# Value product of a key block cut in two halves of its query columns, in an attention and expert kernel on one Trainium2 core

## The chip, the cores and the metric

The kernel runs on one core of one Trainium2 chip. The metric is the device time of one execution in microseconds (us); lower is better. TensorE (PE in the profile) does the matrix products, PEld is its weight load, VectorE is DVE, ScalarE is ACT, GpSimd is POOL, SyncE is SP (SPq is its queue of DMA issues).

## What is computed

`x` is 8 x 1024 tokens of 256 numbers. It is normalised, and three things are added: the input, an attention layer, and a feed-forward layer of eight experts (two chosen per token) with one shared expert. The change lies in the attention. Cut to that:

```python
xn = layernorm(x)
Q, K, V = [(xn @ W + b).reshape(8, 1024, 16, 16) for W, b in ((Wq, bq), (Wk, bk), (Wv, bv))]
scores = einsum('bqhd,bkhd->bhqk', Q, K) * 16 ** -0.5 + alibi       # alibi: slope of the head * (k - q)
attn = softmax(scores, axis=-1)
out = einsum('bhqk,bkhd->bqhd', attn, V).reshape(8, 1024, 256) @ Wo + bo
y = x + out + experts(xn) + shared(xn)
```

## The kernel before

All five engines run the same walk through the work, `Order.run` (L78): each engine's class overrides the steps in which it has something to do, and semaphores tie them together. So the order in which `Order` calls the steps is the order of instructions on each engine.

**Stages.** First the tokens are normalised and projected (16 groups of 512 tokens, up to about 225 us). Then comes the attention, then the experts in 71 blocks of 256 tokens, then the shared expert with the output projection.

**The attention** goes over 64 pairs: a pair `r` is two heads of one batch entry (8 entries, 16 heads). A pair has 8 key blocks `kc` of 128 keys, and `attention(s, n)` with `s = 8 * r + kc` is called for each; it issues work on every second call, for two key blocks at once, by the string `ORDER` (L42). I call the work of one key block a **step**. Its letters:

- `S`, `scores` (L567): one product of 128 keys by 512 queries, 54 rows deep, for one head `hh` and one half `half` of the 1024 queries. Head 0 sits in rows 0 to 53 of the operands (`QO`, `KO`, both parts of the tile OPS), head 1 in rows 64 to 117. Four `S` per step fill PSUM banks 0 to 3; ScalarE's `exp` (L772) takes two banks at once and writes a 128 x 1024 tile of probabilities into `pta` or `ptb`. A score product of half `n` waits for the `exp` of two halves before, which frees its banks.
- `u`, `max_unit` (L542): one product of 128 queries by 512 keys, 52 rows deep, for the row maxima of a later pair (48 units, 12 steps, ahead). It goes to one of three banks (5, 6, 7) in a ring: `ring_bank` (L528) makes unit `n` wait until VectorE has reduced unit `n - 3` (semaphore `mxred`). VectorE's reduction is L917, four per step. `S` and `u` beside it are for different heads, so for different rows of the array: I call the two a **couple**.
- `P`, `values` (L583): the value product of one key block, two steps behind the scores: four products, one for each head and query half, each 128 keys deep and 32 columns of weights wide, 512 query columns long. Each has its own 32 columns of the array and its own 32 partitions of PSUM bank 4, which sums over the eight key blocks of the pair. The operands are plain 32-bit floats, and every such product stands in the trace as two passes (8 MATMUL records for the four).

The maxima of a pair are finished with a small reduction (L921) and three small GpSimd instructions (L1179, L1182, L1184), transposed on TensorE in `max_rows` (L556, the product of L488) into bank 0, copied by ScalarE (L761) and sent by SP into the operands of the next pair. `max_rows(r + 1)` comes in the two-step call that begins at `kc == 4`; it waits for the `exp` of the first half of key block 5, which frees bank 0. At the end of a pair ScalarE copies bank 4 into `accs` (L779); SP sends the sums of the exponentials to `sq` (L1368), VectorE takes their reciprocals (L926), and SP and GpSimd bring them back and multiply.

The loop of `attention` is the part that the change touches:

```python
ORDER = "SuSuSuSuPSuSuSuSuP"
...
                    if v == 1 and kc == 4 and r + 1 < NPAIR:
                        self.max_rows(r + 1)
                    if s >= 2:
                        self.values(*divmod(s - 2 + v, 8))
                    v += 1
```

Of the kernel before, what the change touches and what calls it, by code (L numbers as in the profile page):

```python
# [20 lines left out]
GT = 512  # L21
# [6 lines left out]
NPAIR = NB * NH // 2  # L28
# [10 lines left out]
PAIR_AT = (3, 6)  # L39
V_AT = 10  # L40
UNITS = (0, 2, 5, 7)
ORDER = "SuSuSuSuPSuSuSuSuP"  # L42
KMAX, KEXP = 52, 54
NPT = 8
SCAT_AT = 34
# [28 lines left out]
class Order:  # L74
# [132 lines left out]
    def attention(self, s, n):  # L207

        r, kc = divmod(s, 8)
        if s % 2 == 0:  # L210
            i = v = 0
            for c in ORDER:
                if c == "S":
                    if r < NPAIR:
                        self.scores(r, kc + i // 4, i % 2, i // 2 % 2)
                    i += 1
                elif c == "u":
                    if n < 32 * NPAIR:
                        self.max_unit(n)
                        n += 1  # L220
                else:
                    if v == 1 and kc == 4 and r + 1 < NPAIR:
                        self.max_rows(r + 1)
                    if s >= 2:
                        self.values(*divmod(s - 2 + v, 8))
                    v += 1
            if kc == 0:
                self.next_pair(r)
            elif r >= 1:
                self.heads(r - 1, kc // 2)  # L230
        if r < NE + 2 and kc == 1:
            self.pack_expert(r)
        if s < NBLK:
            self.clear_slots(s)
        if SCAT_AT <= r < SCAT_AT + NG:
            self.scatter_rows(r - SCAT_AT, kc, 16 * r + 2 * kc)
        if kc == 5 and r % 8 in (2, 3) and r < NPAIR - 8:
            self.load_v(r // 8 + 1, r % 8 - 2)
        if s % 4 == 3:
            self.route(s // 4)  # L240
        return n
# [23 lines left out]
    def load_pair(self, r, i): pass  # L265
    def begin_heads(self): pass
    def scores(self, r, kc, hh, half): pass
    def values(self, r, kc): pass
    def heads(self, r, i): pass
    def pack_expert(self, e): pass  # L270
    def clear_slots(self, s): pass
# [46 lines left out]
def build(nc, t, out):  # L318
    ctx = ExitStack()
    with ctx:  # L320
        sem = {n: ctx.enter_context(nc.semaphore("s_" + n)) for n in SEMS}
# [7 lines left out]
        ps = ctx.enter_context(nc.psum_tensor("ps", [P, 8, 512], F32))  # L329
# [39 lines left out]
        vb = VB[:, :].rearrange("p (b c n) -> p b c n", b=2, c=8)  # L369
# [68 lines left out]
        def pt(n):  # L438
            s = n % NPT
            return pta[:, s, :] if s < NPT // 2 else ptb[:, s - NPT // 2, :]  # L440
# [10 lines left out]
        def projections_over(w):  # L451

            w.wait_ge("lgc", NG)
            w.wait_ge("vmm", 4 * NG)
            w.wait_ge("wol", 1)
            for k in range(2):
                w.wait_ge(f"qh{k}", 16 * NG // 2)
                w.wait_ge(f"ql{k}", 16 * NG // 2)
                w.wait_ge(f"vs{k}", 16 * NG // 2)
            for k in range(3):  # L460
                w.wait_ge(f"xn{k}", 16 * len(range(k, NG, 3)))
# [8 lines left out]
        class Tensor(Order):  # L470
# [109 lines left out]
                if hh == 1:  # L580
                    q.then_inc(sem["smm"], 1)

            def values(self, r, kc):  # L583
                b, j = divmod(r, NH // 2)
                n = 16 * r + 2 * kc
                self.w.wait_ge("exp", n + 2)
                self.w.wait_ge("vcp", 2 * b + 2)
                if kc == 0:
                    self.w.wait_ge("acc1", r)
                    self.w.wait_ge("vev", 4 * NG)  # L590
                for hh in range(2):
                    for half in range(2):
                        g4 = 2 * hh + half
                        q = self.mm(ps[32 * g4:32 * g4 + 32, 4, :],
                                    vb[:, b % 2, kc, 32 * (2 * j + hh):32 * (2 * j + hh) + 32],
                                    pt(n + half)[:, hh * GT:(hh + 1) * GT], kc == 0, kc == 7)
                q.then_inc(sem["pv"], 1)

            def route(self, i):
                if i != 15:  # L600
# [112 lines left out]
        class Scalar(Order):  # L713
# [57 lines left out]
                self.w.wait_ge("smm", n + 1)  # L771
                self.e.activation(pt(n), ps[:, b:b + 2, :], ACT.Exp).then_inc(sem["exp"], 1)  # L772

            def values(self, r, kc):
                if kc == 7:
                    projections_over(self.w)
                    self.w.wait_ge(f"ox{r % 2}", 16 * (r // 2))
                    self.w.wait_ge("pv", 8 * (r + 1))
                    self.e.copy(accs[:, r % 2, :], ps[:, 4, :]).then_inc(sem["acc1"], 1)  # L779
# [699 lines left out]
```

## Time and profile before

| | |
|---|---|
| median of 3 runs | 2723.81 us (2722.07 to 2725.03) |
| the profiled execution | 2719.96 us, span 2717.9 us, mean granted clock of TensorE 0.982 |
| TensorE, matmuls | 2527.5 us busy, 93% of the span |
| VectorE | 2114.4 us, 78% |
| ScalarE | 1639.8 us, 60% |
| GpSimd | 858.1 us, 32% |
| L917, reductions of maxima | 2048, 1270.6 us busy, 681 ns each |
| L475, value products | 4096 records, 555.9 us busy |

"Busy" of an engine is the time in which at least one of its instructions runs. Matmuls are pipelined, so that many overlap; their ends are modelled. The number in brackets behind an instruction is the idle time of its engine before it, and what ended it.

### The profile page before, as it was taken

To read this page: it belongs to the slowest core of one execution; us is meant where nothing else is said; L and a number is where in the kernel's file an instruction comes from. 1 tells how busy PE (TensorE), PEld (TensorE's weight loads), DVE (VectorE), ACT (ScalarE), POOL (GpSimd) and SP (SyncE) were. 2 spreads that over 40 slices of the span, in tenths; PEclk is the share of its full clock that TensorE was granted. 3 is DMA by queue.
4 is the path that set the end of the run, shared out by engine and by line. 5 is a ranking of instruction groups with operands and counts; after the bars stand their busy time and mean duration, and the time that the engine had idled before them with its cause. 6 is when DMAs were issued, how large, how long until landed. Compare 5 with 4: busy or idle time off the path is not lost.

```text
span 2717.9 us, 42994 instructions
## 1 busy us (share of the span) xinstructions
PE 2527.5 (93%) x16090; PEld 1580.8 (58%) x16090; DVE 2114.4 (78%) x3518; ACT 1639.8 (60%) x2314; POOL 858.1 (32%) x920
## 2 busy tenths in 40 slices
PE   4999989999999999998999999899999999999998
PEld 3774333333333333333333333799999988887887
DVE  7887888999999998888899996677777765555544
ACT  2445666777777776776677777677777752232222
POOL 4333434100101104445441001333333333444333
PEclk8998899999999999999999999999999999999999
DMA  5995555222222224444442221577777753344332
GB/s 187 335 324 198 189 180 175 77 62 62 76 60 72 70 62 125 135 131 128 125 120 70 68 65 59 194 241 242 242 239 239 239 170 94 96 117 110 97 93 78
DMA packets 213359, 383.62 MB, mean 141 GB/s; under 512 B 45264, under 2 KB 134544, under 8 KB 203792
## 3 DMA queue, kind: packets, MB, share of 16 engines
q1 hardware_dynamic: 175040, 218.25, 26.2%
q0 software_dynamic: 37024, 161.83, 18.8%
q8 instruction: 128, 2.10, 0.3%
q10 hardware_dynamic: 1088, 0.79, 0.1%
q14 instruction: 79, 0.65, 0.1%
HBM read 248.84 MB, written 141.43 MB: 144 GB/s over the span
## 4 chain that ended last, share of the span: by engine, by line
PE 62%; DVE 22%; issue 6%; ACT 5%; DMA 4%; SPq 1%; POOL 1%; ACTq 0%; DVEq 0%; POOLq 0%
PE ps L475 60%; DVE mx L917 13%; DVE OPS L1088 3%; ACT pta L772 2%; PE ps L488 2%; DVE VB L1085 2%; DMA sq<-accs 2%; ACT OPS L844 1%; SPq L1347 1%; DVE OL L1074 1%; ACT OPS L826 1%; DMA WR0c<-Wd,widx 1%; DVE VB L1105 0%; DVE xn L891 0%; DMA xt<-in_x 0%
## 5 line engine op out<-in xcount | busy, mean ns | idle before, releaser
L917 DVE TENSOR_REDUCE mx<-ps 128x1 f32<-128x512 f32 x2048 | 1270.6, 681 | 160.2 <-PE ps L475 152.3
L475 PE MATMUL ps<-OPS 54*128 54x512 f32 (+1 forms) x4096 | 897.0, 443 | 89.3 <-DVE mx L917 41.3
L475 PEld LDWEIGHTS ps<-OPS 52*128 52x128 f32 (+1 forms) x4096 | 461.6, 189 | 797.2 <-DVE mx L917 279.3
L772 ACT ACTIVATE pta<-ps 128x1024 f32<-128x1024 f32 x512 | 496.1, 1021 | 254.0 <-PE ps L475 252.4
L772 ACT ACTIVATE ptb<-ps 128x1024 f32<-128x1024 f32 x512 | 496.0, 1022 | 179.5 <-PE ps L475 176.0
L475 PE MATMUL ps<-OPS,WB 128*128 128x256 f32 (+1 forms) x2268 | 363.6, 312 | 6.4 <-issue 2.6
L475 PEld LDWEIGHTS ps<-OPS,WB 128*128 128x128 f32 x2268 | 310.5, 180 | 35.9 <-issue 7.0
L475 PE MATMUL ps<-ptb,VB 128*32 128x512 f32 x2048 | 279.7, 619 | 0.0
L475 PE MATMUL ps<-pta,VB 128*32 128x512 f32 x2048 | 276.2, 612 | 0.0
L475 PE MATMUL ps<-OPS,WB0c 128*128 128x256 f32 (+3 forms) x1440 | 257.9, 330 | 2.8 <-DVE WB0c L1039 1.8
L1191 POOL TENSOR_TENSOR accs<-accs,asum 128x512 f32<-128x512 f32 x64 | 81.8, 1279 | 499.4 <-DMA asum<-Sd 499.4
L475 PEld LDWEIGHTS ps<-OPS,WB0c 128*128 128x128 f32 (+1 forms) x1440 | 210.2, 181 | 33.1 <-issue 3.9
L475 PE MATMUL ps<-WB,OPS 128*128 128x256 f32 (+1 forms) x1422 | 189.3, 284 | 26.8 <-DVE OPS L1088 26.8
L475 PEld LDWEIGHTS ps<-WB,OPS 128*128 128x128 f32 (+1 forms) x1422 | 178.5, 191 | 33.4 <-issue 33.3
L1061 DVE TENSOR_TENSOR OPS<-VB,OPS 128x256 fp32r<-128x256 f32 (+1 forms) x213 | 152.3, 715 | 35.8 <-ACT OPS L814 35.8
L838 ACT ACTIVATE VB<-ps 128x512 f32<-128x512 f32 (+1 forms) x96 | 56.9, 593 | 197.7 <-PE ps L475 197.0
L1227 POOL DMA_INDIRECT Xs<-xr,slot x128 | 126.0, 984 | 120.4 <-DMA xr<-Xn 83.5
L1088 DVE TENSOR_TENSOR OPS<-VB,OPS 128x512 fp32r<-128x512 f32 (+1 forms) x96 | 111.7, 1164 | 65.9 <-ACT OPS L844 36.4
L1099 DVE SCALAR_TENSOR_TENSOR VB<-gath,prob,ps 128x256 f32<-128x256 f32 x64 | 26.5, 475 | 162.5 <-PE ps L475 162.5
L1179 POOL TENSOR_SCALAR m<-m 128x16 f32<-128x16 f32 x64 | 20.0, 312 | 417.8 <-DVE m L921 417.2
L844 ACT CAST OPS<-VB 128x512 fp32r<-128x512 f32 (+1 forms) x96 | 59.6, 620 | 146.3 <-DVE VB L1085 123.0
L1269 POOL DMA_INDIRECT gath<-Ys,slot x128 | 128.1, 1001 | 36.4 <-issue 34.1
(154 smaller groups left out, 2873.8 us busy)
## 6 DMA issues: line engine op xcount, KB each, us to landing
OPS<-QKh SPq DMA_DIRECT2D x512, 64.0 KB
Xs<-zero POOLq DMA_DIRECT2D x71, 256.0 KB, 3.7
xr<-Xs SPq DMA_DIRECT2D x71, 256.0 KB
Ys<-VB SPq DMA_DIRECT2D x71, 256.0 KB
QKh<-qkH SPq DMA_DIRECT2D x16, 1024.0 KB, 5.8
QKl<-qkL SPq DMA_DIRECT2D x16, 1024.0 KB, 8.5
OPS<-QKl SPq DMA_DIRECT2D x256, 64.0 KB
asum<-Sd SPq DMA_DIRECT2D x64, 256.0 KB
```

The costliest lines, as they stand in the source:

```text
L475: return self.e.matmul(o, l, r, start=start, stop=stop)
L488: return self.e.transpose(o, in_, ident[:, :])
L772: self.e.activation(pt(n), ps[:, b:b + 2, :], ACT.Exp).then_inc(sem["exp"], 1)
L838: self.e.activation(sg[0:hn, k, :], ps[0:hn, 2 + 2 * (n % 2), :], ACT.Silu).then_inc(sem["sg"], 1)
L844: self.e.copy(HH[0:hn, s, :], hf[0:hn, k, :]).then_inc(sem["hh"], 1)
L917: e.reduce_max(mx[:, k2, hh, i, half:half + 1], ps[:, bank, :], AX.X).then_inc(sem["mxred"], 1)
L1061: e.tensor_tensor(HL[0:hn, s, 0:BT], hfq[0:hn, k, :], HH[0:hn, s, 0:BT].bitcast(F32), ALU.subtract).then_inc(sem["hl"], 1)
L1085: e.tensor_tensor(hf[0:hn, k, :], ps[0:hn, 3 + 2 * (n % 2), :], sg[0:hn, k, :], ALU.mult).then_inc(sem["hf"], 1)
L1088: e.tensor_tensor(HL[0:hn, s, :], hf[0:hn, k, :], HH[0:hn, s, :].bitcast(F32), ALU.subtract).then_inc(sem["hl"], 1)
L1191: self.e.tensor_tensor(accs[:, r % 2, :], accs[:, r % 2, :], asum[:, :], ALU.mult).then_inc(sem["nrm"], 1)
L1227: e.indirect_dma_start(Xs[:, :], bass.IndirectOffsetOnAxis(ap=slot[:, c, 4 * g + j:4 * g + j + 1], axis=0), xr[:, k, j, :], None).then_inc ...
L1269: self.e.indirect_dma_start(gath[:, j, c, :], None, Ys[:, :], bass.IndirectOffsetOnAxis(ap=slot[:, c, i:i + 1], axis=0)).then_inc(sem[f"ga ...
```

## The change

The value product of a key block is issued in two halves: query columns 0 to 255 of each of the four products, then columns 256 to 511 of each. `ORDER` places the first half behind two couples and the second behind the other two. `values` takes the half `q`; the bank is opened by the first half of the first key block and closed by the second half of the last; the semaphore `pv` is raised by the second half alone. `max_rows` is now called at `v == 2`, ahead of the first half that stands behind two couples of key block 5.

```diff
-ORDER = "SuSuSuSuPSuSuSuSuP"
+ORDER = "SuSuPSuSuPSuSuPSuSuP"
...
-                    if v == 1 and kc == 4 and r + 1 < NPAIR:
+                    if v == 2 and kc == 4 and r + 1 < NPAIR:
                         self.max_rows(r + 1)
                     if s >= 2:
-                        self.values(*divmod(s - 2 + v, 8))
+                        self.values(*divmod(s - 2 + v // 2, 8), v % 2)
                     v += 1
...
-            def values(self, r, kc):
+            def values(self, r, kc, q):
...
                 b, j = divmod(r, NH // 2)
-                n = 16 * r + 2 * kc
+                n, at = 16 * r + 2 * kc, slice(q * 256, q * 256 + 256)
...
-                        q = self.mm(ps[32 * g4:32 * g4 + 32, 4, :],
-                                    vb[:, b % 2, kc, 32 * (2 * j + hh):32 * (2 * j + hh) + 32],
-                                    pt(n + half)[:, hh * GT:(hh + 1) * GT], kc == 0, kc == 7)
-                q.then_inc(sem["pv"], 1)
+                        done = self.mm(ps[32 * g4:32 * g4 + 32, 4, at],
+                                       vb[:, b % 2, kc, 32 * (2 * j + hh):32 * (2 * j + hh) + 32],
+                                       pt(n + half)[:, hh * GT:(hh + 1) * GT][:, at], kc == 0 and not q, kc == 7 and q == 1)
+                if q:
+                    done.then_inc(sem["pv"], 1)
...
-            def values(self, r, kc):
-                if kc == 7:
+            def values(self, r, kc, q):
+                if kc == 7 and q:
```

The order on TensorE in the call that begins at `kc == 4`, from the couples of key block 4 on. OPS rows are score and maxima products (8 of them are four couples), rows with `ptb,VB` or `pta,VB` are value products, the row L488 is the transposition of the maxima. Before:

```order
L475 MATMUL ps<-OPS 128x512 x8
L475 MATMUL ps<-ptb,VB 32x512 x4
L475 MATMUL ps<-OPS 128x512 x8
L488 MATMUL ps<-ident,mneg 32x128
L475 MATMUL ps<-ptb,VB 32x512 x4
L475 MATMUL ps<-OPS 128x512 x8
```

The same place in the change:

```order
L475 MATMUL ps<-OPS 128x512 x4
L475 MATMUL ps<-ptb,VB 32x256 x4
L475 MATMUL ps<-OPS 128x512 x4
L475 MATMUL ps<-ptb,VB 32x256 x4
L475 MATMUL ps<-OPS 128x512 x4
L488 MATMUL ps<-ident,mneg 32x128
L475 MATMUL ps<-ptb,VB 32x256 x4
L475 MATMUL ps<-OPS 128x512 x4
L475 MATMUL ps<-ptb,VB 32x256 x4
```

There is a value product of half the length behind every two couples, and the transposition stands behind two couples of key block 5 where it stood behind four.

On ScalarE, at the same place (L772 is `exp`, L761 the copy of the transposed maxima, L779 that of bank 4). Before:

```order
L772 ACTIVATE ptb<-ps 128x1024 x4
L772 ACTIVATE pta<-ps 128x1024 x4
L761 CAST mT<-ps 32x128
L772 ACTIVATE ptb<-ps 128x1024 x4
L772 ACTIVATE pta<-ps 128x1024 x4
L779 COPY accs<-ps 128x512
```

In the change, whose lines there are two further on:

```order
L774 ACTIVATE ptb<-ps 128x1024 x4
L774 ACTIVATE pta<-ps 128x1024 x3
L763 CAST mT<-ps 32x128
L774 ACTIVATE pta<-ps 128x1024
L774 ACTIVATE ptb<-ps 128x1024 x4
L774 ACTIVATE pta<-ps 128x1024 x4
L781 COPY accs<-ps 128x512
```

The copy of the maxima stands ahead of the second `exp` of key block 5 where it stood behind it. The orders of VectorE, GpSimd and SP are the same as before.

## Rows read from the trace of the kernel before

**Rows 1.** The page: an engine's busy time (share of the span) and its instructions

```profile
PE 2527.5 (93%) x16090; PEld 1580.8 (58%) x16090; DVE 2114.4 (78%) x3518; ACT 1639.8 (60%) x2314; POOL 858.1 (32%) x920
```

**Rows 2.** Busy time by stretch: start:end and length, engines, PEclk, DMA share, GB/s

```profile
806.81:1050.89 244.08, 234.05 (x1422) 91.79 (x1419) 220.59 (x375) 178.31 (x199) 32.69 (x56) 1.00 0.27 74
```

**Rows 3.** Timeline of ScalarE, first `exp` of pairs 0 and 62: start, length, instruction

```profile
233.40 1.02 ACT L772 ACTIVATE pta<-ps 128x1024 f32<-128x1024 f32 x1 [8.04 <-PE ps L475]
...
1669.80 1.02 ACT L772 ACTIVATE pta<-ps 128x1024 f32<-128x1024 f32 x1 [0.78 <-PE ps L475]
```

**Rows 4.** The chain of waits from 984.3 to 1006.5: start, length, what

```profile
1003.49 0.70 DVE mx L917
1004.20 0.04 issue
1004.24 1.95 PE ps L475 x11
1006.19 0.02 issue
1006.21 0.70 DVE mx L917
```

**Rows 5.** Timeline of the step at 1003 us

```profile
1002.95 1.79 PE L475 MATMUL ps<-OPS 54*128 54x512 f32 x8
1003.49 2.48 DVE L917 TENSOR_REDUCE mx<-ps 128x1 f32<-128x512 f32 x4 [0.23 <-PE ps L475]
1003.78 1.94 ACT L772 ACTIVATE ptb<-ps 128x1024 f32<-128x1024 f32 x2 [0.78 <-PE ps L475]
1004.24 0.18 PEld L475 LDWEIGHTS ps<-OPS 52*128 52x128 f32 x1 [0.52 <-DVE mx L917]
1004.67 0.16 PEld L475 LDWEIGHTS ps<-pta,VB 128*32 128x32 f32 x8 [0.25 <-issue]
1004.67 1.06 PE L475 MATMUL ps<-pta,VB 128*32 128x512 f32 x8
1005.66 0.30 PEld L475 LDWEIGHTS ps<-OPS 54*128 54x128 f32 x4 [0.84 <-issue]
```

**Rows 6.** Timeline, 1005.12: second passes of the four value products

```profile
1005.12 0.61 PE L475 MATMUL ps<-pta,VB 128*32 128x512 f32 x4
```

**Rows 7.** Timeline, a step of pair 62 where no maxima products are left

```profile
1679.80 0.73 PE L475 MATMUL ps<-OPS 54*128 54x512 f32 x4
1680.46 1.06 PE L475 MATMUL ps<-ptb,VB 128*32 128x512 f32 x8
1681.48 0.50 PE L475 MATMUL ps<-OPS 54*128 54x512 f32 x2
```

**Rows 8.** Timeline, key block 5 of pair 33, with the transposition

```profile
1019.24 1.78 PE L475 MATMUL ps<-OPS 54*128 54x512 f32 x8
1020.09 1.94 ACT L772 ACTIVATE pta<-ps 128x1024 f32<-128x1024 f32 x2 [0.80 <-PE ps L475]
1021.22 0.09 PEld L488 LDWEIGHTS ps<-ident,mneg 128*32 128x32 f32 x1 [0.51 <-issue]
1021.45 1.06 PE L475 MATMUL ps<-ptb,VB 128*32 128x512 f32 x8
1022.45 0.19 PEld L475 LDWEIGHTS ps<-OPS 54*128 54x128 f32 x2 [0.84 <-ACT mT L761]
```

**Rows 9.** Timeline: end of the maxima of pair 34, and the sums of pair 32

```profile
1011.90 0.59 SPq L1368 DMA_DIRECT2D sq<-accs  x1
1016.87 0.19 DVE L921 TENSOR_REDUCE m<-mx 128x16 f32<-128x32 f32 x1
1016.97 0.24 DVE L926 RECIPROCAL sq<-sq 128x16 f32<-128x16 f32 x1
```

**Rows 10.** Timeline: a reciprocal that waited for its transfer (pair 35)

```profile
1085.66 0.59 SPq L1368 DMA_DIRECT2D sq<-accs  x1
1089.20 0.25 DVE L926 RECIPROCAL sq<-sq 128x16 f32<-128x16 f32 x1 [2.40 <-DMA sq<-accs]
```

**Rows 11.** Waits from 258 to 1669 us: engine, line, waited for: total, times, longest

```profile
PEld ps L475 <- DVE mx L917: 267.1, 457, 3.3
...
DVE sq L926 <- DMA sq<-accs: 17.2, 11, 2.7
```

**Rows 12.** Busy time by stretch, as rows 2, around the longest of those waits

```profile
1245.00:1250.00 5.00, 2.58 (x16) 1.00 (x16) 2.29 (x6) 3.33 (x4) 0.44 (x1) 0.92 0.79 210
1250.00:1255.00 5.00, 4.55 (x17) 1.93 (x17) 3.31 (x6) 0.64 (x1) 3.93 (x7) 0.50 0.24 81
```

More of the change, by code:

```diff
@@ L267, in scores, with values @@
     def scores(self, r, kc, hh, half): pass
-    def values(self, r, kc): pass
+    def values(self, r, kc, q): pass
     def heads(self, r, i): pass
```

## Prediction

> **What bounds the kernel now.** I read the page first, then the busy time by stretch, then the chain of waits, then the timeline of one step, since shares alone do not say which wait ends last.
>
> TensorE is busy 93% of the span, VectorE 78% [rows 1]. In the even part of the attention, pairs 24 to 34, TensorE reads 96% and VectorE 90% [rows 2]: either could be the bound. 244.08 us for 11 pairs is 22.19 us per pair. The whole of pairs 0 to 61 takes 1669.80 - 233.40 = 1436.4 us [rows 3], 23.17 each; the excess of about 1.0 us per pair is extra VectorE work (routing) and waits for transfers, in some pairs only.
>
> The chain of waits shows a loop with a period of 2.71 to 2.72 us, which is one step: a reduction of maxima (0.70), 0.04, then TensorE (1.95), then the next reduction [rows 4]. The timeline shows what is in it [rows 5]. The step's couples begin at 1002.95. The first reduction starts at 1003.49, once its unit is there, and ends near 1004.19. The fourth unit needs the bank that this reduction reads, so its weight load stands until 1004.24. The value product is behind it, at 1004.67, and the next step at 1005.66. So 0.54 (couple to reduction) + 0.70 + 0.05 + 0.43 (the fourth unit alone) + 0.99 (the value product) = 2.71. TensorE counts as busy throughout, but without that wait the fourth unit would have begun with its couple. VectorE idles 0.23 us in each step, ScalarE 0.78: neither is the bound. Both products and the reduction stand in one ring.
>
> **What TensorE's pieces cost.** A value product is 0.99 to 1.02 us from its first load to the next score load [rows 5, 7]. Its second passes start 0.45 us after the first [rows 6]. If 512 columns stream for 0.427 us per pass (my estimate: two cycles a column at 2.4 GHz, granted clock 1.00 [rows 2], which fits these 0.45), streaming is 0.85 and 0.14 is fixed: the first load, and the array running empty before it takes other rows. Two couples with nothing to wait for, from their first load to that of the value product, are 1680.46 - 1679.80 = 0.66 us [rows 7].
>
> **The change, part by part.**
>
> 1. *The wait of the fourth unit.* In the new order a half product (over 0.5 us) lies between the second and the third couple. The fourth unit comes at about 0.66 + 0.57 + 0.34 = 1.57 us after the step's start, and the reduction that it waits for has ended at 0.54 + 0.70 = 1.24. The wait is gone. Next in line are TensorE's own work and VectorE's four reductions.
>
> 2. *VectorE's floor.* Four reductions take 2.48 us, the last being 0.68 [rows 5]: they start 0.60 apart, so a step can't be under 2.40 us.
>
> 3. *TensorE's work.* A half product has half the columns and all of the fixed part: 0.43 + 0.14 = 0.57. No row shows one. Bounds: half of the whole, 0.50; or, if the loads of the second passes (each 0.11 long) no longer hide beside a pass of 0.21 us, 0.68. I take 0.57: rows 5 has all eight loads done within 0.16 us of the product's start, far ahead of the second passes, and this is less than the new pass. A step is then 2 x 0.66 + 2 x 0.57 = 2.46 us, with TensorE the bound just above VectorE's 2.40. Against 2.71 that is 0.25 less. The bounds give 2.40 (VectorE's floor) and 2.68.
>
> In this place the Trainium skill speaks against the change. "TensorEngine Tiling (Array Packing)", Tiling Modes, Key Properties, says that changing the tiling mode drains TensorE; the kernel changes between two row tiles and four column tiles twice a step, and will do so four times. The rows agree that a change costs: two couples take 0.66 where the spacing of couples would give less, and the product has its 0.14. With free changes the sum would be at VectorE's 2.40 per step; with the rule it is 2.46, as above.
>
> 4. *The transposition of the maxima, once per pair.* It waits for the `exp` of the first half of key block 5, and only two couples now cover that wait. Before: the step starts at 1019.24, that `exp` runs from 1020.09 to 1021.11, the transposition loads at 1021.22, the value product at 1021.45, the next step at 1022.45 [rows 8]: 3.20 us, 0.49 over a normal step. After: the `exp` starts at the same distance, since its scores are the first two couples, so TensorE stands at the same 2.21 us from the step's start when the first half product may load, but two couples and a half product are still to come: 2.21 + 0.57 + 0.66 + 0.57 = 4.01 us, 1.55 over a normal step. The move costs 1.06 us per pair. The maxima themselves are ready in time: the reduction L921 starts at 1016.87 [rows 9], and 4.35 us to the transposition shrink by 0.2 at most. On ScalarE the copy of the maxima now stands ahead of the second `exp` of the block, whose scores come over 1 us after the transposition; SP's transfer behind it keeps more than two steps until its scores. Both at nothing.
>
> 5. *VectorE in key block 4.* The reduction L921 and the reciprocal L926 (about 0.38 us together, as they displace L917) were mostly covered by its 0.23 of idle time. Now there is 0.06. Between 0 and 0.32 I take 0.15 per pair.
>
> 6. *Twice the value instructions, none more elsewhere.* Their columns are counted; issue is hidden, as eight loads and four matmuls of a product start within 0.16 us [rows 5]. The accumulation and `pv` end where they did, so `accs` and the probability tiles come free at the same point.
>
> **Sum.** A pair: 7 x 2.46 + 4.01 + 0.15 = 21.38, against 22.19: 0.8 us less. Pairs 0 to 61: 50 us. Where the reciprocal waited for its transfer (11 times, 17.2 us [rows 11]), the shorter steps ahead only lengthen the wait, by about 0.5 us: 5 us back. In the last 12 steps there are no units; there each half product is paid in full and nothing is won: 0.2 us x 12 = 2 us back. Net 42 to 43 us. The profiled execution (2719.96) becomes about 2677.5; the median of the runs lies 3.85 us above that execution, so **2681 us**, 1.6% less.
>
> **The rivals.**
>
> *A. VectorE becomes the bound.* If the half product costs 0.50, the step is 2.40 and a pair 7 x 2.40 + (2.21 + 0.50 + 0.66 + 0.50) + 0.38 = 21.05. 1.14 x 62 = 71, less 5: 2658. For it: fixed parts may overlap. Against: both whole products in rows 5 and 7 show them. Chance 0.10.
>
> *B. The sums of the exponentials come too late.* The read of `sq` is issued at 1011.90, the reciprocal runs at 1016.97 [rows 9], in front of key block 4's reductions; the new steps leave about 4.6 us in place of 5.07. Where it waited, the transfer took 3.5 us [rows 10], so 1 us is left. If the transfer needs longer in many pairs, up to 0.5 us per pair goes: 31 us of the gain, 2712. In a long wait the clock falls too: 0.92, then 0.50 in the next 5 us [rows 12], the lower of its two levels. Chance 0.07.
>
> *C. Slower: the half product is dearer.* Its place is the value product, 16 halves per pair. What is won otherwise is 0.8 us per pair, so it decides from 0.57 + 0.8 / 16 = 0.62 us. With 0.68 the step is 2 x 0.66 + 2 x 0.68 = 2.68, key block 5 2.21 + 0.68 + 0.66 + 0.68 = 4.23, the pair 22.99: 0.8 x 62 = 50 us slower, and 5 + 5 more at the end and in the waits: 2784. For it: sixteen records must pass where there were eight, and one load unhidden is enough. Against: the loads stand early in rows 5. The Trainium skill has the rule in "TensorE: Matmul & The Clock Gate", Part 3: a weight load overlaps running matmuls only where its row group differs. The value products use all rows, so by it the second loads would be exposed. The trace does not agree for the whole product: its eight loads are done long before the second passes. Chance 0.13.
>
> *D. The order is not what it says.* Excluded: the rows of the order show a half product behind every two couples, and the transposition moved.
>
> **How the numbers follow.** The forecast, 2668 to 2700 around 2681, has 0.66, A 0.10, B 0.07, C 0.13; 0.04 is for a half product between 0.60 and 0.64 us, where little changes either way. The range reaches from A to the near side of C: 2655 to 2730. Under 0.2% (5.4 us) this kernel's measurement can't tell a change from none. Forecast, A and B are faster; half of the in-between case and the near edge of C are not to be told: faster 0.80, same 0.06, slower 0.14.
>
> **What would show it.** Steps of 2.46 us in the middle of a pair and 4.0 at key block 5; the wait of TensorE's loads for L917 (267.1 us [rows 11]) down to less than a quarter; a half product of 0.57 us from load to load; VectorE's share in pairs 24 to 34 up from 90% to some 94%. Wrong would be: steps of 2.6 us or more with few waits (rival C), waits for `sq` in most pairs (B), reductions back to back (A), or a transposition that stands for another reason than its `exp`.

## The result and the profile after

The changed kernel takes 2805.36 us (median of 4 runs, 2800.40 to 2814.01) against 2723.95 us before (4 runs on the same chip): 3.0% **slower**, ratio 1.0303, 95% interval 1.0277 to 1.0329. The forecast was 2681 us, faster, with a range up to 2730. The sign was wrong.

The page of the changed kernel gives engines, TensorE's granted clock in 40 slices, and the costliest groups (lines after L42 are two further on: L919 is the reduction L917 of before, L774 is `exp`):

```profile
PE 2609.3 (93%) x20186; PEld 1578.6 (56%) x20186; DVE 2123.4 (76%) x3518; ACT 1691.9 (60%) x2314; POOL 861.0 (31%) x920
...
PEclk8998788889889999899998999799999999999999
...
L919 DVE TENSOR_REDUCE mx<-ps 128x1 f32<-128x512 f32 x2048 | 1275.2, 684 | 245.4 <-PE ps L475 229.7
```

TensorE's share is still 93% [rows 1], of a longer span, and VectorE's has fallen, not risen. The row of the clock has many 8 and two 7 between slices 4 and 26, where the attention lies; a mean share of busy time doesn't show that, since a slower matmul counts as busy for longer. The mean granted clock went from 0.982 to 0.933 (0.937 or 0.938 in the other three executions, which were not the ones profiled).

I looked first at whether the wait that was to go had gone. The chain of waits in a quiet pair (57) and the sums of waits from 233 to 1760 us answer that:

```profile
1645.14 0.61 ACT pta L774
...
1646.06 0.59 ACT accs L781
...
1646.69 6.27 PE ps L475 x59
...
1652.98 1.32 PE ps L475 x12
...
1654.38 1.03 ACT pta L774
1655.42 0.14 issue
1655.55 0.27 PE ps L488
1655.82 8.43 PE ps L475 x80
```

```profile
DVE mx L919 <- PE ps L475: 217.9, 259, 2.5
...
PE ps L488 <- ACT pta L774: 74.2, 59, 1.5
...
PEld ps L475 <- ACT accs L781: 41.6, 54, 1.1
...
PEld ps L475 <- DVE mx L919: 38.7, 65, 3.3
```

The ring of rows 4 is gone: TensorE now runs for 6 to 8 us at a time, and its loads wait 38.7 us for the reductions in place of 267.1 [rows 11]. The new wait is that of L488, the transposition, for the `exp`: 74.2 us over 59 pairs, 1.26 us each. The second new one is for the copy into `accs`: 41.6 us over 54 pairs. The timeline of the same pair shows this second wait in its first line, and then the pieces of a half step:

```profile
1646.69 0.16 PEld L475 LDWEIGHTS ps<-pta,VB 128*32 128x32 f32 x8 [0.79 <-ACT accs L781]
...
1649.17 0.16 PEld L475 LDWEIGHTS ps<-pta,VB 128*32 128x32 f32 x8 [0.37 <-issue]
1649.17 0.64 PE L475 MATMUL ps<-pta,VB 128*32 128x256 f32 x8
...
1649.74 0.30 PEld L475 LDWEIGHTS ps<-OPS 54*128 54x128 f32 x4 [0.41 <-issue]
...
1650.41 0.16 PEld L475 LDWEIGHTS ps<-pta,VB 128*32 128x32 f32 x8 [0.37 <-issue]
```

A half product is 1649.74 - 1649.17 = 0.57 us and two couples 1650.41 - 1649.74 = 0.67: a step of 2.48 us, where 2.46 was worked out. So far the change does what was forecast. What went wrong is behind the transposition. This is the timeline of pair 58:

```profile
1675.41 0.74 PE L475 MATMUL ps<-OPS 54*128 54x512 f32 x4
1676.25 1.02 ACT L774 ACTIVATE pta<-ps 128x1024 f32<-128x1024 f32 x1 [0.36 <-PE ps L475]
1677.39 0.10 PEld L488 LDWEIGHTS ps<-ident,mneg 128*32 128x32 f32 x1 [1.60 <-issue]
1677.42 0.27 PE L488 MATMUL ps<-ident,mneg 128*32 128x128 f32 x1 [1.26 <-ACT pta L774]
...
1678.86 1.08 PE L475 MATMUL ps<-ptb,VB 128*32 128x256 f32 x8
...
1679.86 0.50 PEld L475 LDWEIGHTS ps<-OPS 54*128 54x128 f32 x4 [0.81 <-issue]
...
1681.01 0.20 PEld L475 LDWEIGHTS ps<-pta,VB 128*32 128x32 f32 x8 [0.65 <-issue]
```

From about 1678.9 us on a half product lasts 1.00 us and two couples 1.15: the lower clock, 1.2 GHz. The same in stretches (columns as in rows 2), then the whole pair, then the pair behind it:

```profile
1676.00:1677.40 1.40, 0.16 (x2) 0.01 (x1) 1.35 (x3) 1.02 (x1) 0.00 (x0) 1.00 0.00 0
1677.40:1678.50 1.10, 1.08 (x11) 0.54 (x13) 0.00 (x0) 0.25 (x1) 0.00 (x0) 1.00 0.05 15
1678.50:1683.00 4.50, 4.50 (x28) 1.40 (x24) 2.71 (x5) 2.05 (x2) 0.00 (x0) 0.54 0.14 47
1683.00:1688.70 5.70, 5.70 (x48) 1.99 (x48) 4.54 (x8) 3.65 (x4) 1.27 (x1) 0.76 0.25 81
...
1663.93:1688.71 24.78, 23.16 (x195) 8.44 (x196) 20.28 (x35) 17.03 (x19) 1.95 (x4) 0.86 0.24 72
1688.71:1710.58 21.87, 20.25 (x195) 7.65 (x196) 20.08 (x35) 17.05 (x19) 1.69 (x4) 1.00 0.17 47
```

TensorE has nothing to do for 1.3 us, and 1.5 us after the gap its clock is halved for some 7 us, in which it is busy without a break and so the bound. The pair takes 24.78 us; its neighbour, with the same wait and no fall, 21.87. Over the attention (first `exp` of pair 0 to that of pair 62, pairs 10 to 23, pairs 51 to 61, and the rest) the changed kernel shows:

```profile
235.31:1753.75 1518.44, 1404.04 (x11943) 519.34 (x11945) 1275.67 (x2161) 1054.74 (x1116) 372.59 (x543) 0.90 0.33 98
506.87:862.27 355.40, 328.94 (x2706) 120.11 (x2702) 294.80 (x506) 238.32 (x252) 36.38 (x65) 0.88 0.22 61
1501.55:1753.75 252.20, 234.32 (x2127) 87.21 (x2123) 221.46 (x375) 187.42 (x198) 22.68 (x46) 0.95 0.21 59
1753.75:1803.52 49.77, 48.11 (x329) 14.43 (x325) 11.22 (x20) 34.21 (x37) 8.66 (x10) 0.64 0.30 111
```

and the kernel before, in the same stretches:

```profile
233.40:1669.80 1436.40, 1342.05 (x7990) 528.89 (x7988) 1266.96 (x2161) 1005.20 (x1117) 368.73 (x540) 0.98 0.35 103
486.97:806.81 319.84, 297.75 (x1809) 116.94 (x1806) 291.02 (x506) 227.00 (x252) 36.77 (x64) 1.00 0.24 68
1425.78:1669.80 244.02, 233.99 (x1422) 91.87 (x1419) 220.60 (x375) 178.33 (x199) 23.09 (x46) 1.00 0.22 62
1669.80:1706.57 36.77, 31.61 (x201) 9.76 (x202) 10.98 (x20) 31.60 (x36) 7.88 (x9) 1.00 0.37 135
```

Between the two profiled executions lie 94 us: 82 more in pairs 0 to 61, 13 more in the last two, where the clock is 0.64, and 1 less elsewhere. (The medians are 81 us apart: the profiled execution of the changed kernel is the slowest of its four.) The granted clocks of pairs 0 to 61, 0.98 and 0.90, mean some 60 us at 1.2 GHz before and some 300 after.

### The profile page after: what moved, and what is told of

It is laid out like the page before. It is cut to its first block, busy times and chain, and to the rows that moved or that the text cites. A ratio compares the mean times of both kernels' runs of the same rounds, so it can differ in the third digit from the quotient of the medians.

```text
span 2812.2 us, 51186 instructions
## 1 busy us (share of the span) xinstructions
PE 2609.3 (93%) x20186; PEld 1578.6 (56%) x20186; DVE 2123.4 (76%) x3518; ACT 1691.9 (60%) x2314; POOL 861.0 (31%) x920
## 4 chain that ended last, share of the span: by engine, by line
PE 73%; DVE 12%; ACT 7%; issue 4%; DMA 1%; POOL 0%; SPq 0%; ACTq 0%; DVEq 0%; POOLq 0%
PE ps L475 71%; DVE mx L919 4%; ACT pta L774 4%; DVE OPS L1090 3%; PE ps L488 2%; DVE VB L1087 2%; ACT accs L781 1%; ACT OPS L846 1%; DVE OL L1076 1%; ACT OPS L828 1%; DVE VB L1107 0%; DVE xn L893 0%; DMA sq<-accs 0%; SPq L1349 0%; DMA xt<-in_x 0%
## 5 line engine op out<-in xcount | busy, mean ns | idle before, releaser
L919 DVE TENSOR_REDUCE mx<-ps 128x1 f32<-128x512 f32 x2048 | 1275.2, 684 | 245.4 <-PE ps L475 229.7
L475 PE MATMUL ps<-OPS 52*128 52x512 f32 (+1 forms) x4096 | 873.4, 485 | 18.7 <-DVE mx L919 17.1
L475 PEld LDWEIGHTS ps<-OPS 52*128 52x128 f32 (+1 forms) x4096 | 369.7, 201 | 542.1 <-issue 477.2
L774 ACT ACTIVATE pta<-ps 128x1024 f32<-128x1024 f32 x512 | 523.9, 1025 | 244.7 <-PE ps L475 226.7
L774 ACT ACTIVATE ptb<-ps 128x1024 f32<-128x1024 f32 x512 | 525.3, 1027 | 208.8 <-PE ps L475 202.0
L475 PE MATMUL ps<-pta,VB 128*32 128x256 f32 x4096 | 366.5, 433 | 21.9 <-ACT accs L781 21.2
L475 PE MATMUL ps<-ptb,VB 128*32 128x256 f32 x4096 | 359.5, 427 | 0.0
L475 PEld LDWEIGHTS ps<-pta,VB 128*32 128x32 f32 x4096 | 84.8, 113 | 236.3 <-issue 194.1
L475 PEld LDWEIGHTS ps<-ptb,VB 128*32 128x32 f32 x4096 | 84.2, 112 | 172.8 <-issue 166.3
```

Source lines behind the costliest of these rows:

```text
L475: return self.e.matmul(o, l, r, start=start, stop=stop)
L919: e.reduce_max(mx[:, k2, hh, i, half:half + 1], ps[:, bank, :], AX.X).then_inc(sem["mxred"], 1)
```

## The experiments

The theory that I began with: the wait at the transposition brings TensorE's clock down, by itself, and that turns a gain into a loss. The rivals: the halves do it by themselves, wherever the transposition is, or only the two together. Every ratio is against the kernel before on the same chip, with its 95% interval; the medians of different experiments come partly from different chips, on which the kernel before takes 2717 to 2724 us. The clocks given for a whole kernel are those of the profiled execution.

**Transposition late again (e1_late).**

```diff
-                    if v == 2 and kc == 4 and r + 1 < NPAIR:
+                    if v == 3 and kc == 4 and r + 1 < NPAIR:
```

> The change with one edit: the transposition of the maxima stands behind four couples of key block 5 again, ahead of the second half product of that block, so that the exp it waits for is covered. Theory (the idle stretch of TensorE before the transposition lets its clock fall, all else won): key block 5 takes 3.0 to 3.3 us in place of 4.0, the mean granted clock returns to 0.975 or more, even pairs take 20.9 to 21.4 us, the time is 2660 to 2690 us, faster than before. Rival (the halves themselves keep TensorE too little occupied, or cost too much): the clock stays under 0.95 and the time over 2760 us.

Measured: 2687.28 us, ratio 0.9879 (0.9856 to 0.9902). With this one digit changed it is faster than before. Mean clock 0.970, where 0.975 or more was expected. Key block 5 takes 3.22 us, quiet pairs 21.09. Pairs 10 to 23 and 51 to 61 of this kernel:

```profile
487.28:791.54 304.26, 291.10 (x2706) 111.08 (x2702) 288.87 (x506) 236.72 (x252) 36.81 (x64) 1.00 0.24 72
1402.92:1634.94 232.02, 223.59 (x2127) 84.56 (x2123) 220.40 (x375) 186.15 (x198) 23.40 (x46) 1.00 0.21 65
```

In these pairs the halves alone don't lower the clock. What remains below 1.00 lies elsewhere: in pairs 0 to 7 and 35 to 44, mostly behind waits for transfers, and in the last pair. There it is lower than before (0.96 over pairs 0 to 61, against 0.98).

**The move alone (e2_move_alone)**, whole products:

```diff
-ORDER = "SuSuSuSuPSuSuSuSuP"
+ORDER = "SuSuSuSuPSuSuMSuSuP"
...
+                elif c == "M":
+                    if kc == 4 and r + 1 < NPAIR:
+                        self.max_rows(r + 1)
                 else:
-                    if v == 1 and kc == 4 and r + 1 < NPAIR:
-                        self.max_rows(r + 1)
```

> The kernel before, value products whole, with the transposition alone moved behind two couples of key block 5. Theory (the stall lowers the clock): key block 5 takes about 3.9 us at the higher clock, and the clock falls behind it in many pairs; mean granted clock under 0.96, time 2790 to 2840 us. Rival (only the halves lower the clock): the stall costs its 0.7 us per pair alone, clock 0.975 or more, time 2755 to 2775 us.

Measured: 2765.39 us, ratio 1.0188 (1.0161 to 1.0216), clock 0.980. Here my theory fell, and the rival's number came out: the same wait, 1.26 us, beside whole products costs its own time (key block 5 3.86 us) and little of the clock. Pairs 10 to 23 and 51 to 61:

```profile
487.23:824.10 336.87, 293.49 (x1809) 113.00 (x1806) 301.46 (x507) 230.32 (x253) 37.20 (x65) 1.00 0.21 64
1455.78:1708.16 252.38, 231.72 (x1422) 89.34 (x1419) 221.68 (x375) 180.96 (x199) 23.47 (x46) 0.99 0.19 60
```

Little is not nothing. Within 2 us of the gap the clock fell, for 3.4 us each time, in seven of the 38 pairs from 24 to 61 (pair 61: 24.01 us at 0.93, where its neighbour takes 22.86), and this profile is the fastest of the four executions; the others have 0.971 to 0.977. Neither part does by itself what the change does, so the theory from here on is that the wait and the spread halves do it together.

**Halves together (e3_adjacent)**, the transposition where it was before:

```diff
-ORDER = "SuSuPSuSuPSuSuPSuSuP"
+ORDER = "SuSuSuSuPPSuSuSuSuPP"
```

> The change with both half products of a key block behind its four couples, and the transposition where it stood before: the cut alone, with no more switches between score and value products. If the fixed 0.14 us is paid per switch, the two halves together take about 1.0 us, a step stays at 2.71 us and the time at 2720 to 2730 us. If it is paid per product, they take 1.14 us, a step 2.85 us and the time is 2785 to 2800 us. In both cases the fourth unit waits for the reduction as before.

Measured: 2716.29 us, ratio 1.0002 (0.9992 to 1.0012). Its timeline of TensorE:

```profile
1002.45 1.79 PE L475 MATMUL ps<-OPS 54*128 54x512 f32 x8
1004.16 1.07 PE L475 MATMUL ps<-pta,VB 128*32 128x256 f32 x16
1005.16 1.20 PE L475 MATMUL ps<-OPS 54*128 54x512 f32 x7
```

16 records of 256 columns take the 1.00 us of 8 records of 512. The cut by itself is free; the fixed 0.14 us is paid per switch between score and value products. The Trainium skill ("TensorEngine Tiling (Array Packing)", Tiling Modes, Key Properties) says that changing the tiling mode drains TensorE. The trace agrees that a change costs: two half products apart take 2 x 0.57 = 1.14 us, together 1.00.

**Halves together, and the move (e10_adjacent_move)**: e3's order, with the transposition behind two couples (`"SuSuSuSuPPSuSuMSuSuPP"`).

> Halves as in the change, but together behind four couples (as e3_adjacent), and the transposition behind two couples of key block 5 (as e2_move_alone). Theory (it is the spreading of the halves, with its twice as many switches, that thins TensorE's work, not the cut): as e2_move_alone, 2755 to 2775 us, clock 0.975 or more. Rival (more and shorter instructions are enough): clock under 0.96, over 2785 us.

Measured: 2777.77 us, ratio 1.0206 (1.0174 to 1.0237), clock 0.973. Near e2_move_alone, 0.002 of the clock and 3 us outside what was expected of the theory, and far from the changed kernel. Pairs 10 to 23 and 51 to 61:

```profile
495.17:833.18 338.01, 297.12 (x2705) 143.19 (x2702) 299.46 (x505) 230.33 (x252) 37.08 (x64) 0.99 0.22 64
1471.30:1729.06 257.76, 237.68 (x2126) 114.89 (x2123) 221.87 (x375) 180.97 (x199) 22.91 (x46) 0.97 0.21 58
```

So most of the loss of clock needs the spreading, but not all of it. In pairs 24 to 61 the number of falls at this gap hardly differs: nine of 38 here, seven in e2_move_alone, ten in the changed kernel. Their length does: 3.4 us in six of the nine here, 6.8 to 13.7 us in eight of the ten there. In pairs 10 to 23, where VectorE has more to do, the clock falls in two of fourteen here, in none in e2_move_alone, in ten in the changed kernel. In these profiles the gap by itself brings falls; the spread halves make them longer and, in the busier pairs, frequent.

**Whole density next to the wait (e7_dense).** Key blocks 4 and 5 have their halves together, the other six apart; the wait stays.

```diff
+DENSE = "SuSuSuSuPPSuSuMSuSuPP"
...
-            for c in ORDER:
+            for c in DENSE if kc == 4 and r < NPAIR else ORDER:
...
+                elif c == "M":
+                    if r + 1 < NPAIR:
+                        self.max_rows(r + 1)
```

> The change, with its long wait at the transposition kept behind two couples of key block 5, but with the halves of key blocks 4 and 5 together behind four couples, so that only the products next to the wait are as dense as in the kernel before; the other six blocks keep the halves apart. Key block 5 should take 2.21 + 0.66 + 1.00 = 3.9 us, a pair about 22.0 us. Theory (the clock falls where the wait and the thinner work of the halves lie next to each other): mean granted clock 0.97 or more, time 2725 to 2760 us. Rival (the halves in the whole pair bring TensorE down, wherever the wait is): clock under 0.95, time over 2790 us.

Measured: 2757.54 us, ratio 1.0146 (1.0122 to 1.0171), clock 0.966 in place of 0.97 or more. Pairs 10 to 23 and 51 to 61:

```profile
498.18:835.85 337.67, 302.13 (x2706) 116.82 (x2702) 297.56 (x506) 236.78 (x253) 37.52 (x65) 0.95 0.23 65
1467.41:1711.38 243.97, 224.05 (x2127) 85.91 (x2123) 222.50 (x375) 186.21 (x199) 23.33 (x47) 1.00 0.22 62
```

In pairs 51 to 61 the clock no longer falls (in pairs 24 to 26 it still does, for 3.4 us each); in pairs 10 to 23, where routing work on VectorE holds TensorE up besides, it still does at times, less than in the changed kernel (0.95 against 0.88). Work next to the wait counts, but not it alone.

**A shorter wait (e8_behind_half).** As the change, but the transposition stands behind the first half product of key block 5, not ahead of it.

```diff
-                    if v == 2 and kc == 4 and r + 1 < NPAIR:
-                        self.max_rows(r + 1)
                     if s >= 2:
                         self.values(*divmod(s - 2 + v // 2, 8), v % 2)
+                    if v == 2 and kc == 4 and r + 1 < NPAIR:
+                        self.max_rows(r + 1)
                     v += 1
```

> The change with the transposition behind the first half product that follows two couples of key block 5, not ahead of it: the wait is 0.57 us shorter. Key block 5 should take 1.98 + 0.23 + 0.66 + 0.57 = 3.45 us. Theory (it is the length of the idle stretch that brings the clock down with the halves): clock 0.96 or more, time 2700 to 2730 us. Rival (any wait there does it): clock near 0.935, time over 2770 us.

Measured: 2683.03 us, ratio 0.9852 (0.9829 to 0.9875), clock 0.973; key block 5 takes 3.44 us. That is 17 us under the lower end of what I expected. The gain over the changed kernel, 122 us, is far more than the 0.57 us per pair by which the wait is shorter (35 us): 0.70 us of idle TensorE are left before the transposition in place of 1.26, and in pairs 24 to 61 no fall follows within 2 us of it.

**The wait filled with work (e11_filler).** Ahead of the transposition five copies of the next maxima product are issued into that unit's own bank. They add nothing to the result.

```diff
+                        if n < 32 * NPAIR:
+                            self.filler(n)
                         self.max_rows(r + 1)
...
+            def filler(self, n):
...
+                bank = self.ring_bank("max", n)
+                for _ in range(5):
+                    self.mm(ps[:, bank, :], QO[h0:h0 + KMAX, k, i * P:(i + 1) * P],
+                            KO[h0:h0 + KMAX, k, half * GT:(half + 1) * GT], True, True)
```

> The change as it is, with five extra products (copies of the next maxima unit, into its own bank, read by nobody) ahead of the transposition: TensorE works through the 1.3 us in which it waited for the exp. They add no result and take about 1.1 us of that wait. Theory (the clock falls because TensorE stands idle there): key block 5 stays at 4.0 to 4.2 us, the mean granted clock returns to 0.97 or more, time 2725 to 2760 us, 45 us or more under the change. Rival (something else in that place costs the clock): 2795 us or more, clock under 0.95.

Measured: 2727.89 us, ratio 1.0025 (1.0009 to 1.0041), clock 0.974: some 76 us less than the changed kernel by the two ratios (77 by the medians), for 310 products more. Key block 5 is even 0.16 us longer, 4.16 us. All of pairs 0 to 61, pairs 51 to 61, and the last two pairs:

```profile
233.74:1682.68 1448.94, 1402.31 (x12253) 549.76 (x12255) 1276.46 (x2161) 1055.10 (x1117) 371.04 (x541) 0.97 0.35 103
...
1440.62:1682.68 242.06, 237.54 (x2182) 93.57 (x2178) 220.61 (x375) 187.32 (x199) 23.57 (x47) 1.00 0.22 63
1682.68:1719.45 36.77, 33.11 (x329) 11.53 (x325) 11.02 (x20) 32.80 (x36) 7.38 (x9) 1.00 0.38 136
```

For pairs 0 to 61 this run settles it: same order, the transposition as late, no idle TensorE in front of it, and near the transposition the clock falls in one of pairs 24 to 61 in place of ten, and in one of pairs 10 to 23 in place of ten. It settles nothing for the last two pairs. Pair 62 gets no filler, as no maxima units are left; its transposition stands behind an idle stretch of 1.27 us in both kernels. In the changed kernel the clock fell there, 0.6 us after the transposition began, and stayed at 0.50 to the end of the attention; here it stayed at 1.00.

**The last steps (e4_tail).** e1_late, with the halves together where no maxima units are left (`for c in ORDER if n < 32 * NPAIR else TAIL`, `TAIL = "SuSuSuSuPPSuSuSuSuPP"`).

> As e1_late, and in the last 12 steps, which have no maxima units, the two halves stand together behind four couples of scores. Theory (there halves apart only cost TensorE time and its clock): 2 to 12 us under e1_late, with the higher clock from 1755 us of the changed kernel's span on. Rival (e1_late already keeps the clock there): within 3 us of e1_late.

Measured: 2678.12 us, ratio 0.9857 (0.9840 to 0.9873), 9 us under e1_late, though its interval overlaps that of e1_late. The stretch that was changed is only 1.0 us shorter in the profiles (38.2 against 39.2 us), and its clock is 0.91 in place of 0.90, so the higher clock did not come back there. The rest lies in pairs that the edit doesn't touch, and I can't count it as won.

**The transfer of the sums (e5_recip, e9_best, e12_before_late, e6_before_recip).** In e1_late the step of key block 4 takes 6.3 to 7.7 us in six pairs. The timeline of VectorE in pair 35 shows why:

```profile
1033.52 0.19 DVE L923 TENSOR_REDUCE m<-mx 128x16 f32<-128x32 f32 x1
1037.28 0.25 DVE L928 RECIPROCAL sq<-sq 128x16 f32<-128x16 f32 x1 [3.57 <-DMA sq<-accs]
1037.45 2.41 DVE L919 TENSOR_REDUCE mx<-ps 128x1 f32<-128x512 f32 x4
```

The reductions stand behind a reciprocal whose input has not landed. e5_recip is e4_tail with one more edit: it issues the reciprocal, and SP's transfers behind it, one call later; e6_before_recip is the kernel before with that edit.

```diff
-                if i == 1:
+                if i == 2:
                     self.w.wait_ge("asd", 16 * (r + 1))
                     self.e.reciprocal(sq[:, :], sq[:, :]).then_inc(sem["rcp"], 1)
```

> As e4_tail, and the reciprocal of the sums with the transfers behind it is issued one call of two key blocks later, so that VectorE does not stand for the transfer in front of the maxima. Theory (shorter steps turned slack of that transfer into waits, with low clock behind the longest): waits of L926's reciprocal for its transfer in the attention under 5 us outside the last pairs, 15 to 35 us under e4_tail: 2643 to 2663 us. Rival (other transfers or GpSimd's chain behind them wait instead): within 8 us of e4_tail.

> The kernel before with the later reciprocal alone. In the kernel before 13 waits cost VectorE some 19 us in the attention, outside the last pairs. Theory: 10 to 25 us faster than before, less than the same edit gives e4_tail, whose steps are shorter. Rival (the sums come late elsewhere): no faster than before.

Measured: e5_recip 2684.29 us, ratio 0.9861 (0.9840 to 0.9883), level with e4_tail, as the rival had it; e6_before_recip 2713.86 us, 0.9975 (0.9960 to 0.9989), 8 us gained by the medians where 10 were the least expected. The waits of e5_recip from 990 to 1400 us show the new place:

```profile
PEld ps L489 <- POOL mneg L1187: 28.6, 11, 5.6
```

In pairs 34 to 49 GpSimd issues the scattering of rows, and the maxima of the next pair, which GpSimd has to finish, come late there (11 waits). So e9_best is e4_tail with the later reciprocal only outside those pairs (and not for the last three), and e12_before_late is the kernel before with that same rule:

```diff
+def late(r):
+    return r < SCAT_AT - 1 or SCAT_AT + NG <= r < NPAIR - 3
...
-                if i == 1:
+                if i == 1 + late(r):
```

> As e4_tail, with the reciprocal of the sums one call later only outside pairs 34 to 50, in which GpSimd scatters rows and the later reciprocal of e5_recip held up the maxima behind it. From the starts of the pairs in both profiles: 20 to 27 us under e4_tail and e5_recip, 2650 to 2665 us. Rival (waits of other pairs grow instead): within 8 us of e4_tail.

> The kernel before with the same placing of the reciprocal as e9_best (later outside pairs 34 to 50), as the measure of what that edit gives without the halves. In the profile of the kernel before VectorE waited some 19 us for that transfer, about half of it in the pairs where it is moved. Theory: 5 to 20 us under before, so that 35 us or more of e9_best's gain of 53 us belong to the halves. Rival (the reciprocal makes most of the gain): 30 us or more under before.

Measured: e9_best **2663.16 us**, ratio 0.9807 (0.9778 to 0.9836), the fastest of all; e12_before_late 2703.76 us, ratio 0.9936 (0.9914 to 0.9957), 14 us less than before. So of the 56 us that e9_best gains by the medians, some 42 belong to the halves with the transposition kept late and the last steps as in e4_tail; by the ratios it is 35 of 52.

The table sums up the attention. "10 to 23" and "51 to 61" are us per pair and the granted clock in them, from the busy time by stretch of each profile:

| kernel | ratio | mean clock | pairs 10 to 23 | pairs 51 to 61 |
|---|---|---|---|---|
| before | 1 | 0.982 | 22.85, 1.00 | 22.18, 1.00 |
| the change | 1.0303 | 0.933 | 25.39, 0.88 | 22.93, 0.95 |
| wait filled (e11) | 1.0025 | 0.974 | 23.47, 0.99 | 22.01, 1.00 |
| shorter wait (e8) | 0.9852 | 0.973 | 22.44, 0.99 | 21.31, 1.00 |
| transposition late (e1) | 0.9879 | 0.970 | 21.73, 1.00 | 21.09, 1.00 |
| dense beside the wait (e7) | 1.0146 | 0.966 | 24.12, 0.95 | 22.18, 1.00 |
| move alone, whole (e2) | 1.0188 | 0.980 | 24.06, 1.00 | 22.94, 0.99 |
| halves together, move (e10) | 1.0206 | 0.973 | 24.14, 0.99 | 23.43, 0.97 |

## Why the prediction was wrong

**Part 1, the wait of the fourth unit: right.** 38.7 us are left of 267.1 [rows 11].

**Parts 2 and 3, the step: right.** 2.46 us was forecast, 2.48 measured; the half product is 0.57 us, the value taken between 0.50 and 0.68, and rival C with its dearer half is refuted. The weight loads of the second passes stay hidden in passes of half the length: the half product would be longer otherwise. One sign of success did not come: VectorE's share was to rise to some 94% in pairs 24 to 34, and is 88% there (222.31 of 253.78 us). With free switches the prediction had VectorE's 2.40 us per step; e3_adjacent shows that the fixed part is indeed paid for the switch.

**Part 4, the transposition: its time right, its consequence missed. This is the step that failed.** "The move costs 1.06 us per pair" was right within 0.03: key block 5 takes 4.00 us where the clock holds (4.01 forecast), 1.52 over its neighbours, and took 0.49 over them before. But the move was priced as time only. I had rows 12, where a long wait halves the clock, and used them for rival B alone; the new idle stretch in front of the transposition, 1.26 us in each pair, stands nowhere in the sum, and its effect on the clock was put at nothing without a reason. Beside whole products that is nearly so (e2_move_alone, clock 0.980, falls of 3.4 us in seven of pairs 24 to 61). With the halves spread, TensorE has a switch after every two couples, and the same gap brings the clock down in 10 of the 14 pairs from 10 to 23 and in 3 of the 11 from 51 to 61, mostly for 6.8 us or more. e11_filler puts the price of that at some 76 us; in the profiles it is 70 in pairs 0 to 61 (1518.44 - 1448.94). That is most of the 82 us which the changed kernel loses there. The 13 us of the last two pairs (49.77 - 36.77) go with a fall of the clock too, but no run shows what set it off, since e11_filler has the same gap in pair 62 and no fall.

**Part 5, VectorE in key block 4:** in a quiet pair the step is 2.57 us where 2.61 was forecast. Right there. In pairs 10 to 23, where VectorE has routing work, the moved transposition costs more than the sum says, with the clock up: e2_move_alone takes 24.06 us per pair against 22.85, 1.21 more, while its quiet pairs with the clock up take some 0.67 more (22.86 against 22.19). A likely reading is that VectorE stands idle behind the gap as well (its reductions of pair 58 resume after 1.38 us) and has less room to catch up there; no run isolates it.

**Part 6, "`accs` and the probability tiles come free at the same point": true, and yet wrong in its effect.** The next pair's first value product now comes earlier, behind two couples of key block 2, and has to wait for the copy of bank 4: [0.79 <-ACT accs L781] before its load at 1646.69 us, 0.42 more than the usual 0.37. From score load to score load key block 2 takes 2.90 us, and its neighbours 2.48. With the 0.02 us by which the other steps are over 2.46, a quiet pair without a fall of the clock is 21.88 us and not 21.38. That is 31 us over 62 pairs.

**The sum.** "50 us" for pairs 0 to 61 was really 19 (22.19 - 21.88 = 0.31 per pair) in the quiet case, and less in pairs 10 to 23, so even without the clock the change as made would have been near zero: e11_filler, at 1.0025, says as much. **The waits for the sums**, "5 us back", did not come in the changed kernel: from 233 to 1760 us the reciprocal waits 6.0 us in 3 waits, against 17.2 us in 11 before [rows 11]. They come once the transposition is late again: 29.8 us in 16 waits in e1_late up to the last pairs, with falls of the clock behind the longest. There rival B's mechanism is at work, with 12.6 us more of waiting; in the changed kernel it is not. I did not follow up what makes the difference. **The last 12 steps**, "2 us back", cost 13 in the profiles, with the clock at 0.64 in that stretch; this may be particular to the one profiled execution, as the last two pairs are at 0.90 to 1.00 in all the other profiles, whole products or halves.

None of the rivals was the cause of this result. The one that should have been there: the new idle stretch in front of the transposition, priced at the lower clock.

What stays open: why the clock falls in one quiet pair and not in the next with the same order, why the falls last longer beside spread halves, and how much of the work around a gap counts. e2_move_alone, e7_dense and e10_adjacent_move lie between the clear cases, and I have no run that separates the density of the work before the gap from that behind it.

## What to carry to other kernels

When a change opens a gap in TensorE's work, price it twice: as time, and as a possible fall of the clock behind it; and look at the density of the work around it, since the same gap cost mainly its own time beside whole products (1.9% in all), and beside spread halves some 76 us on top, more than the halves had won. When an order is rewritten, each step that hangs on a position in it (here the transposition and the first product of a pair) has to be looked at again for what covers its wait; cutting a product in two was worth 1.2 to 1.5% as soon as the transposition stood behind enough work. If a gap can't be closed, filling it with idle products is a cheap test of whether the clock is the cause.

## What was not expected of the hardware

- A gap of 1.26 us (pair 58) was followed by 7 us at half clock, while gaps of the same length in e2_move_alone left the clock at 1.00 in pairs 10 to 23 and were followed by 3.4 us at half clock in seven later ones. How long a gap may be is thus no fixed number in these runs.
- Extra work made the kernel faster: 310 products more, some 76 us less.
- Four products of 256 columns in two passes each cost half of those of 512 to within 0.01 us when they stand together (1.00 us for both halves), and 0.07 us more each when they stand apart.
